# The cosine stage of a two-layer decoder block: the context's side computed in an earlier stage and kept in DRAM, norms as columns, and the clamp as a minimum on GpSimd

## The reference

```
v = einsum('bsd,hd->bsh', x, Wv) + bv          # 16 x 128 x 64
t = einsum('bsd,hd->bsh', ctx, Wt) + bt        # 16 x 128 x 64
dots = einsum('bih,bjh->bij', v, t)            # 16 x 128 x 128
denom = maximum(norm(v)[:, :, None] * norm(t)[:, None, :], 1e-8)
x = x + dots / denom
```

## Time and profile before

| what | us |
|---|---|
| median of 3 runs | 833.73 |
| lowest and highest of them | 829.64, 834.97 |
| the profiled execution | 829.35 |
| its span, first to last instruction | 827.0 |
| PE busy in the span | 616.5 |
| VectorE busy | 502.5 |
| ScalarE busy | 382.2 |
| GpSimd busy | 222.0 |

### The profile page before, as it was taken

How to read it: one execution, slowest core, us unless ns; L and a number is a source line. 1 busy time by engine, 2 the same in 40 slices (tenths; PEclk the granted TensorE clock), 3 DMA queues, 4 the chain that set the end, 5 groups by cost and what they waited for, 6 DMA issues and landing times. The chain is left out here.

```text
span 827.0 us, 17075 instructions
## 1 busy us (share of the span) xinstructions
PE 616.5 (75%) x6330; PEld 459.4 (56%) x6360; DVE 502.5 (61%) x1325; ACT 382.2 (46%) x826; POOL 222.0 (27%) x321
## 2 busy tenths in 40 slices
PE   3895998989999854008999428899999856755875
PEld 1463555556666544007998416678787734543554
DVE  3453656477878748533444274857575643788995
ACT  5473764777776531204344515253534235533432
POOL 3131323343534204732445520313131300000000
PEclk9798999999999975558999858999999975566797
DMA  3012234332112110143566220000000000000000
GB/s 95 2 42 76 76 100 120 90 100 76 47 45 85 41 35 27 49 163 125 201 208 214 75 63 1 2 2 2 2 2 2 2 7 25 14 1 0 13 13 25
DMA packets 52830, 46.85 MB, mean 57 GB/s; under 512 B 10203, under 2 KB 45597, under 8 KB 52749
## 3 DMA queue, kind: packets, MB, share of 16 engines
q1 hardware_dynamic: 46845, 39.54, 15.9%
q0 software_dynamic: 2496, 4.27, 1.6%
q10 hardware_dynamic: 3408, 1.97, 0.9%
HBM read 17.13 MB, written 15.01 MB: 39 GB/s over the span
## 5 line engine op out<-in xcount | busy, mean ns | idle before, releaser
L567 ACT ACTIVATE ptx<-bank 128x512 f32<-128x512 f32 x128 | 66.1, 603 | 98.0 <-PE bank L480 97.9
L1483 POOL COPY ptx<-over_pt 32x512 f32<-32x512 f32 x64 | 38.9, 607 | 137.9 <-DVE over_pt L1453 135.1
L1056 POOL DMA_INDIRECT results<-moe_y,moe_dest x46 | 45.2, 983 | 59.1 <-DVE moe_y L1193 51.5
L721 DVE SCALAR_TENSOR_TENSOR ptx<-ptx,bank 128x512 f32<-128x512 f32 x64 | 41.1, 683 | 25.2 <-PE bank L489 23.4
L706 DVE TENSOR_REDUCE l_m<-bank 128x4 f32<-128x512 f32 x64 | 40.9, 678 | 19.6 <-PE bank L464 19.6
L476 PE MATMUL bank<-ke 32*128 32x512 f32 x256 | 37.4, 651 | 19.2 <-issue 15.5
L380 POOL TENSOR_TENSOR x<-x,l_back 128x128 f32<-128x128 f32 x32 | 14.5, 454 | 132.4 <-ACT l_back L580 121.2
L1383 ACT ACTIVATE ke<-bank 64x512 f32<-64x512 f32 x64 | 37.9, 592 | 15.5 <-PE bank L1314 14.7
L996 ACT ACTIVATE moe_h<-bank,ptx 128x256 f32<-128x256 f32 x48 | 19.8, 470 | 53.5 <-PE bank L931 53.4
L680 DVE BATCH_NORM_STATS2 l_stats<-x 128x6 f32<-128x128 f32 x32 | 9.3, 290 | 54.2 <-POOL x L380 54.2
L706 DVE TENSOR_REDUCE l_m_raw<-bank 128x4 f32<-128x512 f32 x64 | 40.7, 673 | 0.1
(11 more groups left out here) (336 smaller groups left out, 1655.9 us busy)
## 6 DMA issues: line engine op xcount, KB each, us to landing
slots<-blank SPq DMA_DIRECT2D x16, 528.0 KB, 4.8
ptx<-w SPq DMA_DIRECT2D x12, 578.0 KB, 3.3
ke<-w SPq DMA_DIRECT2D x11, 578.0 KB, 3.3
w<-in_w SPq DMA_DIRECT2D x16, 256.0 KB
moe_xb<-slots SPq DMA_DIRECT2D x23, 132.0 KB
x<-in_x SPq DMA_DIRECT2D x4, 256.0 KB, 5.6
w<-results SPq DMA_DIRECT2D x4, 256.0 KB, 5.9
w<-results ACTq DMA_DIRECT2D x4, 256.0 KB, 5.8
```

The costliest lines, as they stand in the source:

```text
L567: nc.scalar.activation(probs[t % 2][:, g, :], score_bank[g][:, :], ACT.Exp, scale=SCALE0).then_inc(s["probs"], 1)
L721: nc.vector.scalar_tensor_tensor(probs[t % 2][:, g, :], probs[t % 2][:, g, :], 1.0, floor_bank[g][:, :], ALU.min, ALU.max).then_inc(s["cli ...
L1056: nc.gpsimd.indirect_dma_start(M.results, bass.IndirectOffsetOnAxis(dest[j % 4][:, n:n + 1], 0), y[j % 4][:, n, :], None, bounds_check=2 * ...
L1483: nc.gpsimd.tensor_copy(ptx[t % 2][r, :, r], pt[t % 2][r, :, :]).then_inc(s["spread"], 1)
```

## The change

Three things. First, all that concerns the context moves out of `cosine_block` into the routing stage: SP loads the whole context at the stage's start into a free part of `ke`; after the counts TensorE turns it, projects it, and sums the squares into one column per sequence; ScalarE copies, squares, adds the bias and takes the roots; VectorE floors and inverts these norms; TensorE turns the inverses into rows; ScalarE's queue stores the projections (0.5 MB) and the inverses (16 x 128) to DRAM. `batch_attention` gets a program for SP that loads them back, the inverses broadcast to all lines, with the remaining weights and bias, into buffers that exist from then on. Second, in `cosine_block` the sums of squares are made per row of x as columns (the squares are the stationary operand, a column of ones moves), in full float32 without the doubled weights; the clamp of the product of norms becomes a minimum of the product of inverses with 1e8, made on GpSimd as one TENSOR_SCALAR per sequence. Third, the block is written out, with pairs of buffers in PSUM and SBUF, in a new order, and the row statistics are written out without the small memsets.

In the routing stage (TensorE, then ScalarE, then VectorE):

```diff
+                sp.dma_start(ctx_rows, d["ctx"].rearrange("b p c -> p b c")).then_inc(s["ctx_load"], 16)
+                sp.dma_start(cos_wt[:, :], d["cos_wt"][:, 0:HC]).then_inc(s["ctx_load"], 16)
+                sp.dma_start(cos_bias[:, :], d["cos_bias"][0:HC, :]).then_inc(s["ctx_load"], 16)
                 sp.wait_ge(s["table"], 3)
...
+                def turn_context(q):
+                    if q == 0:
+                        pe.wait_ge(s["ctx_load"], 48)
+                        pe.wait_ge(s["xt"], NB)
+                        pe.wait_ge(s["exps"], NB)
+                    for j in range(4):
+                        mm = nc.tensor.transpose(ctx_bank[q][0:C, j * S:(j + 1) * S], ctx_rows[:, 4 * q + j, :], M.ident[:, :])
+                    mm.then_inc(s["ctx_ps"], 1)
+
+                def project_context(q):
+                    wait(pe, s["ctx"], q, plus=1)
+                    nc.tensor.matmul(ctx_bank[q][0:HC, :], cos_wt[:, :], ctx_turned[:, q, :], start=True, stop=True).then_inc(s["ctt_ps"], 1)
+
+                def context_sums(q):
+                    wait(pe, s["csq"], q, plus=1)
+                    for j in range(4):
+                        mm = nc.tensor.matmul(csum_bank[:, 4 * q + j:4 * q + j + 1], csq[q % 2][:, j * S:(j + 1) * S], M.ones[0:HC, 0:1], start=True, stop=True)
+                    mm.then_inc(s["csum_ps"], 1)
...
                 def down(j):
+                    if j == 0:
+                        pe.wait_ge(s["cturned"], 1)
...
                 mm.then_inc(s["counts"], 1)
+                for q in range(NB):
+                    turn_context(q)
+                for q in range(NB):
+                    project_context(q)
+                    if q > 0:
+                        context_sums(q - 1)
+                context_sums(NB - 1)
+                pe.wait_ge(s["cinv"], 1)
+                nc.tensor.transpose(csum_bank[0:B, S:2 * S], cinv[:, :], M.ident[:, :]).then_inc(s["cturn_ps"], 1)
                 turned(0)
+                pe.wait_ge(s["ctt"], NB)
+                pe.wait_ge(s["csq"], NB)
...
+                for q in range(NB):
+                    wait(act, s["ctx_ps"], q, plus=1)
+                    nc.scalar.activation(ctx_turned[:, q, :], ctx_bank[q][0:C, :], ACT.Copy).then_inc(s["ctx"], 1)
+                for q in range(NB):
+                    wait(act, s["ctt_ps"], q, plus=1)
+                    wait(act, s["csum_ps"], q, plus=-1)
+                    nc.scalar.activation(csq[q % 2], ctx_bank[q][0:HC, :], ACT.Square, bias=cos_bias[:, 1:2]).then_inc(s["csq"], 1)
+                    nc.scalar.activation(ctt[:, q, :], ctx_bank[q][0:HC, :], ACT.Identity, bias=cos_bias[:, 1:2]).then_inc(s["ctt"], 1)
+                act.wait_ge(s["csum_ps"], NB)
+                nc.scalar.activation(cnorm[:, :], csum_bank[:, 0:B], ACT.Sqrt).then_inc(s["cnorm"], 1)
                 for n in range(3):
                     nc.scalar.activation(M.over_hi[:, n, :], M.over_w[:, n, :], ACT.Copy).then_inc(s["high"], 1)
+                act.wait_ge(s["cturn_ps"], 1)
+                nc.scalar.activation(cturned[:, :], csum_bank[0:B, S:2 * S], ACT.Copy).then_inc(s["cturned"], 1)
+                act.wait_ge(s["ctt"], NB)
+                act.dma_start(M.context_rows, ctt).then_inc(s["cstore"], 16)
+                act.wait_ge(s["cturned"], 1)
+                act.dma_start(M.context_inv, cturned[:, :]).then_inc(s["cstore"], 16)
                 for j in range(J):
                     gelu(j)
                 act.wait_ge(s["sum"], J)
+                act.wait_ge(s["cstore"], 32)
...
                 blocks()
+                dve.wait_ge(s["cnorm"], 1)
+                V.tensor_scalar(cfloor[:, :], cnorm[:, :], 1e-18, None, ALU.max).then_inc(s["cfloor"], 1)
+                dve.wait_ge(s["cfloor"], 1)
+                V.reciprocal(cinv[:, :], cfloor[:, :]).then_inc(s["cinv"], 1)
                 for n in range(3):
                     dve.wait_ge(s["high"], n + 1)
```

In `batch_attention`:

```diff
+            @block.sync
+            def _(sp):
+                sp.dma_start(M.cos_tt[:, :].rearrange("p (q n) -> p q n", q=4), M.context_rows).then_inc(s["cosine"], 16)
+                sp.dma_start(M.cos_inv[:, :].rearrange("p (b c) -> p b c", b=B),
+                             M.context_inv.rearrange("(a b) c -> a b c", a=1).broadcast_to([S, B, S])).then_inc(s["cosine"], 16)
+                sp.dma_start(M.cos_wv[:, :], d["cos_wv"]).then_inc(s["cosine"], 16)
+                sp.dma_start(M.cos_bias[:, :], d["cos_bias"]).then_inc(s["cosine"], 16)
+                sp.wait_ge(s["cosine"], 64)
```

The core of `cosine_block` as it is after (TensorE, ScalarE's order, GpSimd, VectorE); `biased` squares and adds the bias for x alone, with 64 lines:

```diff
+                def turn(u, p):
+                    wait(pe, s["xn"], u, per=2, plus=2)
+                    wait(pe, s["xt"], u, plus=-1)
+                    for j in range(2):
+                        mm = nc.tensor.transpose(turn_bank[p][:, j * S:(j + 1) * S], xn[p][:, j, :], M.ident[:, :])
+                    mm.then_inc(s["xt_ps"], 1)
+                def project(u, p):
+                    wait(pe, s["xt"], u, plus=1)
+                    wait(pe, s["vt"], u, plus=-1)
+                    wait(pe, s["sq"], u, plus=-1)
+                    nc.tensor.matmul(vt_bank[p][0:HC, 0:2 * S], M.cos_wv[:, 0:HC], xt[p][:, :, :], start=True, stop=True).then_inc(s["vt_ps"], 1)
+                def sums(u, p):
+                    wait(pe, s["sq"], u, plus=1)
+                    wait(pe, s["norm"], u, plus=-1)
+                    for j in range(2):
+                        mm = nc.tensor.matmul(sum_bank[p][:, j:j + 1], sq[p][:, j, :], M.ones[0:HC, 0:1], start=True, stop=True)
+                    mm.then_inc(s["sum_ps"], 1)
+                def products(u, p):
+                    wait(pe, s["vt"], u, plus=1)
+                    wait(pe, s["cosine"], u, plus=-1)
+                    for j in range(2):
+                        b = 2 * u + j
+                        mm = nc.tensor.matmul(dot_bank[p][:, j * S:(j + 1) * S], vt[p][:, j, :], M.cos_tt[:, b * S:(b + 1) * S], start=True, stop=True)
+                    mm.then_inc(s["dot_ps"], 1)
+                for u in range(-2, N):
+                    if valid(u + 1, N):
+                        project(u + 1, (u + 1) % 2)
+                    if valid(u, N):
+                        sums(u, u % 2)
+                        products(u, u % 2)
                     if valid(u + 2, N):
+                        turn(u + 2, u % 2)
...
+                for u in range(-2, N):
+                    if valid(u + 1, N):
+                        biased(u + 1, (u + 1) % 2)
+                    if valid(u, N):
+                        roots(u, u % 2)
                     if valid(u + 2, N):
+                        turned(u + 2, u % 2)
...
+            @block.gpsimd
+            def _(pool):
+                for u in range(N):
+                    p = u % 2
+                    wait(pool, s["inverse"], u, plus=1)
+                    wait(pool, s["cosine"], u, plus=-1)
+                    for j in range(2):
+                        b = 2 * u + j
+                        nc.gpsimd.tensor_scalar(m[p][:, j, :], M.cos_inv[:, b * S:(b + 1) * S], inv[p][:, j:j + 1], 1e8,
+                                                ALU.mult, ALU.min).then_inc(s["limited"], 1)
...
+                def inverses(u, p):
+                    wait(dve, s["norm"], u, plus=1)
+                    wait(dve, s["inverse"], u, plus=-1)
+                    nc.vector.tensor_scalar(floored[p][:, :], norm[p][:, :], 1e-18, None, ALU.max).then_inc(s["floored"], 1)
+                    wait(dve, s["floored"], u, plus=1)
+                    wait(dve, s["limited"], u, per=2, plus=-2)
+                    nc.vector.reciprocal(inv[p][:, :], floored[p][:, :]).then_inc(s["inverse"], 1)
+                def cosines(u, p):
+                    wait(dve, s["limited"], u, per=2, plus=2)
+                    wait(dve, s["dot_ps"], u, plus=1)
+                    nc.vector.tensor_tensor(cosine[p][:, :, :], halves(dot_bank[p]), m[p][:, :, :], ALU.mult).then_inc(s["cosine"], 1)
...
+                for u in range(-3, N + 1):
+                    if valid(u + 3, N):
+                        normalise(u + 3, (u + 3) % 2)
+                    if valid(u - 1, N):
+                        cosines(u - 1, (u - 1) % 2)
+                    if valid(u, N):
+                        inverses(u, u % 2)
+                    if valid(u - 1, N):
+                        add(u - 1, (u - 1) % 2)
+                        statistics(u - 1, (u - 1) % 2)
```

148 lines of the change are left out of this document (44 added, 104 removed).

## The result

| | before | after |
|---|---|---|
| median, us (4 runs each, one chip) | 832.92 | 808.19 |
| lowest to highest, us | 829.64 to 834.97 | 807.06 to 810.21 |
| the profiled execution; its span, us | 829.35; 827.0 | 807.06; 805.3 |
| granted clock over the span | 0.860 | 0.868 |

The ratio is 0.972, with a 95% interval of 0.969 to 0.975. The forecast was 808.0 us. A run more than 1.5% above the fastest of its kernel is left out of the ratios; there is one, in number 3.

What follows compares the result with a forecast made beforehand. The cosine stage, a ring through TensorE with no engine full, was to give back 25.2 us, less 0.5 in routing: 24.7 off 829.35 is 804.7, plus 4.4 to the median 809.0, put down as 808; range 799 to 817.

Steps and rivals of the forecast that it cites:

- the prediction's own signs of being wrong: GpSimd over 1.2 us each; VectorE's add awaiting GpSimd; first turn or gelu over 2 us later; ranks' lateness over 6 us.
- TensorE's ring bounds the step: Cosine stage: project, sums, products, turn, copy, project closes once a step, 3.96 us at 1.2 GHz.
- VectorE 2.8, GpSimd 0.79 each: Cosine step: VectorE's operations sum to 2.8 us; GpSimd's two take 0.79 us each, 1.7 with hand-overs.
- VectorE would not wait over 0.2 us for GpSimd: Cosine stage, a sign of being right: GpSimd at 0.8 us each, with VectorE not waiting for it over 0.2 us.
- The rival of the port: Cosine stage: VectorE and GpSimd hold each other up, step 4.5 us, about 4 us less won, 812; chance 0.1.
- The rival of the clock: Cosine stage: clock goes up, VectorE with GpSimd binds at 2.8 to 3.1 us, total about 801; chance 0.22.
- The price of 30 to 33 us won: Cosine stage at the raised clock: fill some 2 us shorter, seven steps 0.9 to 1.1 us less each.
- The routing stage at +0.5: Routing stage: the moved context work fits the idle gaps; net cost between -2 and +7.6 us, taken as +0.5.
- Every gap is longer than its work by the records: Routing stage: moved work ends at 366 to 372 on ScalarE before 375.32, 365.5 to 371.5 on VectorE before 372.73.
- the rival's own condition: Routing stage gap does not cover: VectorE's 6.04 us lateness is TensorE's, or store delays fetch; 3 to 8 us lost; chance 0.2.
- the hoped-for 2 us: Routing stage: TensorE, busy until just before 371.58, runs first turns and projections at 2.4 GHz, winning up to 2 us.
- From the profile to the median: Whole kernel: 24.7 us off the profiled 829.35 gives 804.7; the median 4.4 higher, 809.0, put down as 808.

Runs made afterwards that it cites:

- number 3: Changed kernel with each turn and the projection done twice per cosine step, as useless work: 802.87 us for three runs, ratio 0.966; the fourth run 816.38 us.
- number 1: Changed kernel with TensorE turning the next tiles ahead of sums and products in the cosine stage: 806.16 us, ratio 0.969.
- number 2: Changed kernel with the clamp (minimum of inverses) on VectorE instead of GpSimd: 805.99 us, ratio 0.969.
- number 6: Changed kernel with an extra 128x256 reciprocal on VectorE in each cosine step, its result unused: 799.14 us, ratio 0.973.
- number 8: Changed kernel with next tiles turned first, one useless projection per cosine step, seven before the first turn, and sums sharing one PSUM bank: 789.38 us, ratio 0.960.
- number 11: The kernel of number 8 with only the seven useless projections at the start, none in each step: 794.20 us, ratio 0.965.
- number 12: Kernel of number 8 with four useless projections ahead instead of seven, and ranks from running sums with one matmul each: 788.36 us, ratio 0.958.
- the first set: Experiments number 1 to number 4, run on one chip beside the kernel before, which took 831.11 us there.
- the second and third: The later two sets of experiments, each on another chip, beside the kernel before, which took 822.32 and 821.8 us there.
- number 4: Changed kernel with the two stores of the context's side issued after the third block's gelus instead of before the first: 811.56 us, ratio 0.976.

## Why the prediction was right, step by step

The time was right, and so was the mechanism of the cosine stage, which gives the whole gain; several terms were off and partly cancelled. That the median came within 0.2 us is luck, as the last paragraph shows. Of the prediction's own signs of being wrong, one appeared: the first turn and the first gelu came 3.0 and 2.6 us later than before, and the limit was 2.

**TensorE's ring bounds the step.** Right at the lower clock: number 1 moved the step by taking one hand-over out, numbers 2 and 6 loaded VectorE and did not move it. The period was put at 3.96 us and is 4.21. The mis-sized term is the products, 0.86 forecast and 1.13 measured (698.20 to 699.33): the other projection from the earlier trace rows, which I took for them, streams the same columns with two loads of weights, the products need four, and PEld shows 0.97 us for these alone. That the loads make the difference is read from these rows; no run varied them by themselves. Projection 1.05 (1.01), sums 0.87 (0.86), turn to copy 0.73 (0.80), copy and hand-over 0.43 (0.43). Six steps times 0.25 is 1.5 us, and the stage gave 23.7 instead of 25.2. The rest cancelled: from the stage's start to the first steady projection it took 5.9 us and not 6.3, and from the last projection to the end 8.5 and not 8.0, where VectorE's last inverses stood behind cosines that waited for GpSimd (717.51, then 717.85).

**VectorE 2.8, GpSimd 0.79 each.** VectorE 2.2 (number 6); the sum counted durations end to end where neighbouring operations overlap by some 0.08 us each. GpSimd's two take 1.53 us alone and 1.61 beside the add, 0.77 to 0.80 each, the row that I chose in the earlier trace rows. It fits, and number 2 shows that it was not needed. That VectorE would not wait over 0.2 us for GpSimd holds for the full steps and not for the last four groups of cosines (0.68).

**The rival of the port.** It did not come: GpSimd started behind VectorE's add, as the order has it, and its two operations took 1.61 us and, where the step is shortest (number 8), 1.70, against 1.53 alone and 1.52 beside number 6's reciprocal (695.29). VectorE's normalising of two tiles, which runs beside GpSimd's second operation, took 0.68 us against 0.60 at the stage's start (687.34). The Trainium skill, page "SBUF — State Buffer", section "Who interferes with whom", calls the shared ports an exclusive lock. By that rule GpSimd would lose the whole overlap with the add, 0.23 us (699.04 to 699.27); the trace shows a cost of 0.08, so it agrees that the two disturb each other and does not show the full exclusion.

**The rival of the clock** had a chance of 0.22 and did not come: 0.50 throughout. But it was nearer than the text thought, and not for the reason given. Numbers 8 and 11 differ by one useless projection a step, and hold 1.00 or fall to 0.50; number 3 came up without the seven ahead. The price of 30 to 33 us won is met by number 8 (31.8 us of stage, 31.5 won) and passed by number 12 (34.4), both with useless work and the other turn order; number 3, at 1.00 in the changed kernel's order, won 28.2. The period in that price, 2.8 to 3.1 us by VectorE, was too long: steps of 2.46 us ran.

**The routing stage at +0.5.** Its pieces were off, and this is the step of the prediction that failed, though the time does not show it. "Every gap is longer than its work by the records" was wrong for this execution: the lateness of 6 us was TensorE's, the rival's own condition, since ScalarE's copy was late with VectorE. The records had TensorE issue its turns at 348.74, but its results came at 354.7. By the prediction's own numbers such a shift makes VectorE's copy late by up to 4.8 us (371.5 + 6 - 372.73), not the 4.3 written there. At the first gelu the cost was 2.6 us less the 1.1 of the later start, 1.5, and not 3 to 8: it is either the store's collision (2.4 more from fetch to turn) or VectorE's low parts (1.8), which exclude each other in these runs, because a later side puts the store behind the fetch. By the next stage's start the shift was 0.6 us, less than the 1.1 at this one's. The +0.5 itself cannot be told from nothing. The clock did not bring the hoped-for 2 us: it was higher in the context's own work (0.61 in the window 345 to 375 us, where it was 0.50), but at the first turns and projections, 372 to 378 us, it was 0.50, where it had been 0.64.

**From the profile to the median.** 21.7 us between spans instead of 24.7: 1.5 from the step, about 1.5 from shifts outside the cosine stage of the size of the spread. The profiled execution, put at 804.7, took 807.06; the median, put at 809.0 and set down as 808, is 808.19, since this time it lies 1.1 above the profiled run and not 4.4. A miss of 2.4 us and these 3.3 us cancelled, with the 1.0 us that was taken off at the end.

## What to carry to other kernels

When a ring through TensorE is to be priced from rows of other operations, count its loads of weights as well as its columns, and count them first when tiles are small. When the granted clock of a stage is at its lower level, removing work from TensorE can be the smaller part of what is to be had: here useless matmuls took the stage of number 1 from 36.4 to 28.9 us (number 12). Try them before taking more away. An engine with a late wait whose releaser is not named should be believed late for every other reader of it, and the cover of moved work be computed from that later time.

## What the runs showed of the hardware

- Adding a projection and two turns to each step of a TensorE-bound ring shortened the step from 4.21 to 3.22 us, since the granted clock rose from 0.50 to 1.00. Without such work the clock fell to 0.50 again within a stretch in which TensorE has no idle time in the records (number 11), and in number 1 it stayed at 0.50 with 10.0 of 10 us recorded busy. A busy share of the page does not foretell the clock.
- The last ranks came 6.8 us after TensorE's first matmul for them in the first comparison and in the first set, and 0.8 to 1.1 us after it in the second and third, on other chips, the changed kernel being in both groups. The kernel before took 831 us in the first set and 822 in the others. Where the ranks are late, TensorE's turns behind them are late too. A trace can so carry a wait of 6 us that another chip does not have.
- A store of 512 KB issued 1.1 us ahead of a fetch of 132 KB on another queue lengthened the time from the fetch's issue to its first use from 2.45 to 4.72 us (number 4 against the changed kernel); a store issued 1.3 us behind the fetch did not (number 1).
- Two TENSOR_SCALAR of 128x128 float32 on GpSimd took 1.53 us alone and 1.61 beside a VectorE add with both inputs in SBUF.
